# One more field by one-hot rows, pair products of a tile in one go, and gathers without marks

## The reference

```python
e  = stack([tbl_f[ids[:, f]] for f in range(26)], axis=1)        # (2048, 26, 32)
x1 = einsum('bik,bjk,hij->bhk', e,  e, W1) + b1[None, :, None]   # h = 128
x2 = einsum('bik,bjk,hij->bhk', x1, e, W2) + b2[None, :, None]
z  = sum(concat([x1, x2], axis=1), axis=-1)                      # (2048, 256)
h  = concat([z, dense_ctx], axis=1)                              # (2048, 272)
h  = maximum(h @ W_top1 + b_top1, 0)                             # 512
h  = maximum(h @ W_top2 + b_top2, 0)                             # 256
y  = h @ W_top3                                                  # (2048, 1)
```

## Time and profile before

| | us |
|---|---|
| median of 3 timed executions | 502.41 (498.45 to 503.1) |
| the profiled execution's own time | 499.69 |
| its span | 497.9 |
| PE busy | 466.3 (94%) |
| DVE busy | 387.7 (78%) |
| POOL busy | 347.6 (70%) |
| ACT busy | 254.4 (51%) |
| mean granted TensorE clock | 0.993 |

### The profile page before, as it was taken

One profiled execution on the slowest core, in us unless ns is written; L12 is line 12 of the kernel. 1 busy time (PEld: TensorE's weight loads), 2 busy tenths in 40 slices (PEclk: granted clock), 3 DMA queues, 4 the chain that ended last, 5 costly groups with the idle time before them and its releaser, 6 DMA issues.

```text
span 497.9 us, 24830 instructions
## 1 busy us (share of the span) xinstructions
PE 466.3 (94%) x10658; PEld 448.1 (90%) x10658; DVE 387.7 (78%) x1143; ACT 254.4 (51%) x531; POOL 347.6 (70%) x274
## 2 busy tenths in 40 slices
PE   4998889869799999999999999999999999999998
PEld 3887879869688998999999999999999999999997
DVE  8699959497596959795979796989779898875302
ACT  7876835375446354544554555546453545455211
POOL 5887978757888878787878787788878788810000
PEclk9999999989999999999999999999999999999999
DMA  6631031120020212020203020202021210000000
GB/s 219 170 105 15 8 66 38 36 54 19 11 65 14 60 13 62 12 58 13 62 11 62 12 58 12 59 14 56 14 34 40 38 35 11 9 5 1 3 0 3
DMA packets 14001, 19.57 MB, mean 39 GB/s; under 512 B 5123, under 2 KB 11528, under 8 KB 13838
## 3 DMA queue, kind: packets, MB, share of 16 engines
q0 software_dynamic: 8512, 4.38, 9.0%
q1 hardware_dynamic: 5454, 14.73, 8.3%
HBM read 19.08 MB, written 0.01 MB: 38 GB/s over the span
## 4 chain that ended last, share of the span: by engine, by line
PE 72%; DVE 14%; issue 4%; DMA 3%; POOL 3%; ACT 3%; SPq 0%; DVEq 0%; ACTq 0%; POOLq 0%
PE psum L939 15%; PE psum L913 15%; PE psum L958 11%; PE psum L984 8%; PE psum L892 6%; DVE work L643 6%; DVE onehot L486 5%; PE psum L1006 4%; POOL emb L396 3%; DMA emb<-in_tbl,idx 3%; PE psum L934 2%; PE psum L835 2%; PE psum L856 2%; PE psum L858 2%; PE psum L979 2%
## 5 line engine op out<-in xcount | busy, mean ns | idle before, releaser
L396 POOL DMA_INDIRECT emb<-in_tbl,idx x266 | 346.7, 1303 | 90.3 <-issue 62.3
L754 ACT COPY t_area<-psum 128x432 f32<-128x432 f32 x256 | 125.2, 541 | 98.2 <-PE psum L913 72.0
L643 DVE TENSOR_TENSOR work<-embT 128x32 f32<-128x32 f32 (+12 forms) x416 | 129.2, 386 | 0.0
L939 PE MATMUL psum<-t_area,v 128*128 (+1 forms) x992 | 113.4, 275 | 0.0
L939 PEld LDWEIGHTS psum<-t_area,v 128*128 128x128 f32 x992 | 112.1, 192 | 0.0
L913 PE MATMUL psum<-diag,work 64*64 64x54 f32 (+1 forms) x6144 | 103.5, 218 | 7.0 <-ACT diag L731 3.6
L913 PEld LDWEIGHTS psum<-diag,work 64*64 64x64 f32 (+1 forms) x6144 | 94.7, 127 | 13.5 <-issue 8.7
L731 ACT COPY diag<-embT 32x416 f32<-32x416 f32 x128 | 69.9, 546 | 29.2 <-DVE embT L625 27.6
L958 PE MATMUL psum<-table_parts,onehot 125*128 125x96 bf16 x1350 | 62.4, 206 | 5.5 <-DVE onehot L486 3.8
L580 DVE COPY t_area<-t_area 13x384 f32<-13x384 f32 (+5 forms) x160 | 61.6, 416 | 6.8 <-ACT t_area L754 5.3
L958 PEld LDWEIGHTS psum<-table_parts,onehot 125*128 125x128 bf16 x1350 | 58.2, 98 | 8.2 <-DVE onehot L486 4.6
(11 more groups left out here) (96 smaller groups left out, 433.1 us busy)
## 6 DMA issues: line engine op xcount, KB each, us to landing
ids_all<-in_short_ids SPq DMA_DIRECT2D x15, 625.0 KB
emb<-in_tbl,idx POOLq DMA_INDIRECT x266
t_area<-in_L_rec_W SPq DMA_DIRECT2D x1, 1664.0 KB, 8.6
work<-in_W_top SPq DMA_DIRECT2D x2, 512.0 KB, 11.9
onehot<-in_tbl SPq DMA_DIRECT2D x5, 156.2 KB
onehot<-in_tbl SPq DMA_DIRECT2D x5, 125.0 KB
t_area<-in_L_rec_W SPq DMA_DIRECT2D x1, 338.0 KB, 4.0
idx<-in_ids SPq DMA_DIRECT2D x1, 208.0 KB, 2.5
```

The costliest lines, as they stand in the source:

```text
L396: eng.indirect_dma_start(emb[n][:, f * K:(f + 1) * K], None, tables[f], bass.IndirectOffsetOnAxis(ap=idx[:, t * F + f:t * F + f + 1], axis=0),
L643: last = nc.vector.tensor_tensor(pairs[:, half, :, :, tri(r):tri(r) + r + 1], halves[:, g, :, 0:r + 1], halves[:, g, :, r:r + 1].broadcast ...
L754: nc.scalar.copy(dst, src).then_inc(t_out, 1)
L939: last = nc.tensor.matmul(z_ps(t)[:, NP:2 * NP], v[:, s, :], moments(slot), start=(a == 0), stop=(a == len(terms) - 1))
```

## The change

`SHORTS` goes from 10 to 11: one more field with 1,250 rows comes by one-hot rows, and 15 gathers a tile are left. Its neighbours in the sorted list are shifted, so the parts of `short_rows` have 48, 44 and 8 matmuls, 100 in all. The third part goes to bank 4 for the first tiles and otherwise to bank 5, in columns behind z.

PE's `step` no longer mixes: all 8 phases of `t_units(t)`, then the three parts of `short_rows(t+1)`, `layer1(t-3)`, `cin(t-1)`, `layer2(t-3)`. `cin` has a new wait for `rows_ready`. On DVE `make_onehot(t+1)` stands behind both halves of the pair products, and `h1_low(t-4)` stands between the halves in place of `h1_low(t-3)` at the end of the tile. On ACT `h1_move(t-3)` comes after all 16 unit copies. The marks and the semaphore `progress` are gone: the gathers of the first 13 fields of tile t start once the first transpose of tile t-2 is done, the others once the second is.

```diff
-SHORTS = 10
+SHORTS = 11
-        def rows_ps(part):
+        def rows_ps(part, t):
+            if part == 2:
+                if isinstance(t, int) and t < 3:
+                    return psum[:, 4, 0:PARTS * K]
+                return psum[:, 5, 2 * NP:2 * NP + PARTS * K]
...
@@ gpsimd
             for t in range(2, TILES):
-                eng.wait_ge(embT_ready, 2 * (t - 1))
-                lo = first if t == 2 else steps[t - 1] - later + AHEAD
-                hi = steps[t - 1] + AHEAD
-                marks = [(prep_full, n) for n in range(AFTER_V1 + 1, PREPS + 1)] if t == 2 else []
-                count = later - len(marks)
-                lo = max(lo, 0 if t == 2 else steps[t - 2] + AHEAD)
-                marks += [(progress, lo + 1 + k * (hi - lo) // count) for k in range(count)]
-                gather(t, marks)
+                for c in range(2):
+                    eng.wait_ge(embT_ready, 2 * (t - 2) + c + 1)
+                    eng.nop(nofuse=True)
+                    gather(t, c)
@@ vector, tile
-                make_pairs(t, n, (lambda: make_onehot(t + 1)) if not known or t + 1 < TILES else None)
+                make_pairs(t, n, (lambda: h1_low(t - 4)) if not known or t >= 4 else (lambda: None))
+                if not known or t + 1 < TILES:
+                    make_onehot(t + 1)
...
-                if not known or t >= 3:
-                    h1_low(t - 3)
@@ scalar, step
-                    for u in range(UNITS // 2):
+                    for u in range(UNITS):
                         unit_out(t, n, u)
                 if not known or 3 <= t < TILES:
                     h1_move(t - 3)
-                if not known or t < TILES:
-                    for u in range(UNITS // 2, UNITS):
-                        unit_out(t, n, u)
@@ tensor, cin
+                if not (isinstance(t, int) and (t == 0 or t >= TILES - 2)):
+                    eng.wait_ge(rows_ready, t + 2)
@@ tensor, short_rows
+                    if part == 2 and not (isinstance(t, int) and t < 3):
+                        eng.wait_ge(z_lo_ready, t - 2)
@@ tensor, step
-                t_units(t, 0)
+                for half in range(2):
+                    t_units(t, half)
+                if not known or t < TILES - 1:
+                    for part in range(len(ROW_PARTS)):
+                        short_rows(t + 1, part)
                 if not known or t >= 3:
                     layer1(t - 3, n)
-                t_units(t, 1)
+                if not known or t >= 2:
+                    cin(t - 1, n)
                 if not known or t >= 3:
                     layer2(t - 3)
-                if not known or t >= 2:
-                    cin(t - 1, n)
```

More of the change, by code:

```diff
@@ L384, in _, with gather @@
                 eng.iota(first_row_int[:, size:size + 1], pattern=[[0, 1]], base=0, channel_multiplier=n).then_inc(rows_known, 1)
-            def gather(t, marks):
+            def gather(t, c=None, marks=None):
                 n = t % 2
-                fields = [f for f in range(F) if f not in SHORT or t == 0]
+                fields = [f for f in range(F) if (f not in SHORT or t == 0) and c in (None, f // HF)]
                 held = None
-                for f, mark in zip(fields, marks):
+                for f, mark in zip(fields, marks or [None] * F):
                     if mark is not None and mark != held:
@@ L403, in _ @@
             later = F - SHORTS
-            gather(0, [None] * EARLY + [(prep_full, AFTER_W2T + 2 * k + 1) for k in range(HF)]
+            gather(0, None, [None] * EARLY + [(prep_full, AFTER_W2T + 2 * k + 1) for k in range(HF)]
                    + [(prep_full, AFTER_MOVED + 2 * k + 1) for k in range(F - EARLY - HF)])
             at = AFTER_MOVED + 2 * (F - EARLY - HF)
-            gather(1, [(prep_full, n) for n in range(at + 1, AFTER_V1 + 1, 2)] + [(t_full, u) for u in range(2, UNITS + 1, 2)]
+            gather(1, None, [(prep_full, n) for n in range(at + 1, AFTER_V1 + 1, 2)] + [(t_full, u) for u in range(2, UNITS + 1, 2)]
                    + [(prep_full, AFTER_V1 + 1)] * later)
-            steps = [sum(marks_in(t) for t in range(u)) for u in range(TILES)]
-            first = len(MARK_PHASES)
             for t in range(2, TILES):
-                eng.wait_ge(embT_ready, 2 * (t - 1))
-                lo = first if t == 2 else steps[t - 1] - later + AHEAD
-                hi = steps[t - 1] + AHEAD
-                marks = [(prep_full, n) for n in range(AFTER_V1 + 1, PREPS + 1)] if t == 2 else []
-                count = later - len(marks)
-                lo = max(lo, 0 if t == 2 else steps[t - 2] + AHEAD)
-                marks += [(progress, lo + 1 + k * (hi - lo) // count) for k in range(count)]
-                gather(t, marks)
+                for c in range(2):
+                    eng.wait_ge(embT_ready, 2 * (t - 2) + c + 1)
+                    eng.nop(nofuse=True)
+                    gather(t, c)
         @block.vector
@@ L492, in make_rows @@
                 for part, fields in enumerate(ROW_PARTS):
-                    eng.wait_ge(rows_full, 2 * (t - 1) + part + 1)
-                    of_field = rows_ps(part).rearrange("p (j a k) -> p j k a", a=PARTS, k=K)
-                    runs = [j for j, f in enumerate(fields) if j == 0 or fields[j - 1] != f - 1] + [PER_BANK]
+                    eng.wait_ge(rows_full, len(ROW_PARTS) * (t - 1) + part + 1)
+                    of_field = rows_ps(part, t).rearrange("p (j a k) -> p j k a", a=PARTS, k=K)
+                    runs = [j for j, f in enumerate(fields) if j == 0 or fields[j - 1] != f - 1] + [len(fields)]
                     for lo, hi in zip(runs, runs[1:]):
@@ L628, in transposes, with make_pairs @@
                 eng.wait_ge(embT_ready, 2 * t + 2)
-            def make_pairs(t, n, between=None):
+            def make_pairs(t, n, between):
                 e = embT[n][:, :, :]
@@ L634, in make_pairs @@
                 for half in range(2):
-                    if half == 1 and between is not None:
+                    if half == 1:
                         between()
@@ L666, in _ @@
             eng.wait_ge(extra_ready, 1)
[L667 removed]
+            make_pairs(0, 0, lambda: None)
             own = split_tables(1, own)
@@ L680, in _ @@
             pack(TILES - 1, 1)
+            h1_low(TILES - 4)
+            z_low(TILES - 2, 0)
             make_y(TILES - 4)
-            z_low(TILES - 2, 0)
             h1_low(TILES - 3)
@@ L870, in t_units @@
                 for v in range(half * phases // 2, (half + 1) * phases // 2):
[L871 to L874, removed]
                     if isinstance(t, int):
@@ L916, in small_units @@
                                 last.then_inc(t_full, 1)
-                    if j == 0 and v in MARK_PHASES:
-                        last.then_inc(progress, 1)
             def cin(t, n):
@@ L957, in short_rows @@
                     for c in range(chunks):
-                        last = nc.tensor.matmul(rows_ps(part)[:, j * PARTS * K:(j + 1) * PARTS * K],
+                        last = nc.tensor.matmul(rows_ps(part, t)[:, j * PARTS * K:(j + 1) * PARTS * K],
                                                 onehot[:, ONEHOT_AT[c] + o - BY_CHUNK[c], :],
@@ L1029, in _ @@
             make_v(AFTER_V1, PREPS)
-            for part in range(2):
+            for part in range(len(ROW_PARTS)):
                 short_rows(1, part)
```

18 lines of the change are left out of this document (1 added, 17 removed).

## The result

| | before | after |
|---|---|---|
| median, 4 executions each | 501.83 us | 507.84 us (505.12 to 509.08) |
| ratio | | 1.0117, 95% interval 1.0076 to 1.0158 |
| profiled execution: time, span | 499.69, 497.9 | 509.08, 506.9 |

The span of the profiled execution grew by 9.0 us, the median time by only 6.0: the changed kernel's profile shows the slowest of its four executions, and the one before is of an execution 2.1 us under its median. So the trace overstates the loss by some 3 us. PE's step starts (the first matmul of `t_units` in each tile) say where. `t_units(3)` starts at 135.7 us (135.5 before), `t_units(4)` at 167.9 (164.6), `t_units(15)` at 457.5 (448.2), and 49.4 us are left (49.7). So tile 3's step, the first of PE's loop, lost 3.1 us, the eleven steady steps (tiles 4 to 14) 6.0 us, start and end together nothing.

A forecast was written before the change was run, and what follows sets the result against it. PE was taken to set the pace, busy 278.87 of 283.6 us in eleven steps. Steady steps +13.2 and start -2.7 gave +10.5 on 499.69, 510.2, or 512.9 on the median; predicted 511.5, range 500 to 519.

The forecast's parts named there:

- Eight phases in a row: PE's t_units: waits for ACT's bank copies before phases 2, 4 and 6; +1.0 us a step, bounds +0.5 and +1.4.
- a quick and a slow kind of tile: Phases 5 to 7 before the change: five tiles at 3.34 to 3.43 us, six at 3.56 to 3.74.
- The field on PE: Ten more one-hot matmuls of 0.045 us each on PE: +0.45 us a step.
- Fewer changes of form: PE switches between quartered and whole matmuls four times less: -0.1 us a step, bounds 0 and -0.3.
- late gathers: 15 gathers without marks fit POOL into PE's step, removing late steady tiles: -0.2 us a step.
- DVE's order: DVE needs 22.8 us before PE gives the next part 0 at 24.7: 2 us to spare, no new wait bites.
- The start: Tiles 1 to 3: 7 us wait before tile 2, tile 3's step ending near 161.9; -2.7 us, bounds 0 and -5.
- The end: Tile 15 and the rest, whole matmuls in nearly the same order: nothing, bounds -1 and +1 us.
- Rival A: ACT's copies never hold PE, eight phases take 7.9 us in all: 492 to 494 us; chance 0.11.
- rival B: All tiles run phases at 9.0 us, +0.45 us a step: 502 us, 505 on the median; chance 0.19.
- Rival C: DVE sets the step if its work stretches by 3 us: each step 1 us longer, 522 us; chance 0.05.
- Rival D: POOL's gathers hang under DVE's products, needing 28.3 us a tile: 520 us; chance 0.05.

The follow-up runs named there:

- half_copy2: Changed kernel, but from tile 4 on each ACT unit copy moves only the first half of its slots (measurement only, z wrong); 499.4 us, ratio 0.9968.
- mix4: Changed kernel with two quarters of layer1 and short_rows part 0 put back between PE's phases, half of layer1 before cin; 498.3 us, ratio 0.9953.

## Why the prediction came out right, and where its sum did not

- **Eight phases in a row** (+1.0 taken, bounds +0.5 and +1.4): +0.48 measured, with the mechanism and the wait's releaser as forecast, and confirmed by half_copy2 and mix4. The first two of its three places show in the trace above, the third lies inside a merged row. I took the mean of a quick and a slow kind of tile; the changed kernel runs near the quick one, 9.2 us for the eight phases where 9.0 and 9.9 were reckoned. The middle was taken, and the truth lay at the lower bound: this is the term of the sum that was mis-sized.
- **The field on PE** (+0.45): 4.42 against 4.04 us, +0.38.
- **Fewer changes of form, late gathers** (-0.1, -0.2): neither was measured by itself. PE's waits for late one-hot columns, 2.3 us in 3 waits before, are gone, which fits the second. With these two as forecast, 0.48 + 0.38 - 0.3 = 0.56 against a measured 26.33 - 25.78 = +0.55 a step, +6.0 in eleven; forecast was +13.
- **DVE's order**: 22.8 us of work with 2 us to spare; the trace shows up to 2.7 us of waiting for part 0 (DVE, line 488). `cin` after tile 2's rows waited 0.73 us (0.8 forecast).
- **The start** (-2.7): +3.3 at tile 4. Its first part was right: a wait of 7.48 us before tile 2 (7 forecast) with a slow clock behind it, and tile 3 at 135.7 (134.8). The step that failed is "its step of 27 us ends near 161.9". It took 32.1, with 4.5 us of gaps without a releaser and 1.5 us of slow clock that the sum has no term for. That code came too slowly for eight phases packed into one stretch, in the loop's first pass, is the likely cause, by timing alone. The trace of before had a small sign of it, a gap of 0.80 us with no releaser in tile 3. The size, too, is that of one execution, the slowest of four: its mean granted clock was 0.987, that of the fastest (505.1 us) 0.993.
- **The end** (0): -0.3.
- **Rival A** (banks do not hold PE) is refuted by the 27 waits, and **rival B** (the quick kind) is nearest to the steady steps. With tile 3's loss the sum came out 1.5 us under the forecast in the profiled executions (+9.0 against +10.5). Two errors of 7 and 6 us cancelled, which was luck: the total was better than its working. On the medians it is +6.0 against a forecast of 511.5 - 502.4 = +9.1.
- **Rival C** did not occur. **Rival D**'s mechanism did: two gathers hung through both halves of the products,

```profile
80.02 8.38 POOL L392 DMA_INDIRECT emb<-in_tbl,idx  x1 [0.30 <-issue]
105.82 7.81 POOL L392 DMA_INDIRECT emb<-in_tbl,idx  x1 [0.30 <-issue]
```

and DVE then waited up to 2.3 us for tile 3's gathers, whose products released PE last (0.38 us). In the steady tiles one gather hangs 3.5 to 4.4 us under most halves of the products, and POOL has the room: a tile's 15 gathers take it some 24 us of PE's 26.3. By the Trainium skill (SBUF — State Buffer, section Who interferes with whom) a `tensor_tensor` should not keep GpSimd from writing descriptors. The page calls that inferred. Here the gathers of 7.81 and 8.38 us lie over products and, at their end, 1.1 us of line 472, with no gap on DVE. The measurement decides, with the mechanism left open.

## What to carry to other kernels

Work that stands between the phases of a producer with few buffers need not be in its way: here it was the time in which the buffers drained (mix4 gained 9.5 us by putting some of it back), so count phases in a row before moving it out. A wait that costs nothing may be covered by one neighbour, and moving the neighbour costs the whole wait (0.84 us a step here). When a change is made of several parts, time them alone: the gathers without marks gained 1%, and the rest of the change lost 2%. When a profile explains a difference, compare its own time with the median first: here 3 of its 9 us were the choice of the execution.

## What was not expected of the hardware

In a loop's first pass pieces of 0.02 MB came on the instruction queue every 3.4 to 5.1 us, and PE, working through 128 quartered matmuls with their weight loads in 2.0 to 2.5 us, stood still until 2.2 to 2.7 us after the next piece began. That it waited for this code is argued from the times, not shown by a run. With a 0.69 MB load on other queues at the same time one piece took 2.1 us instead of 1.0, and one gap was 2.69 us long. After it the granted clock was 0.50 and 100 matmuls took 5.93 instead of 4.42 us; after a gap of 2.40 us in another kernel it was not.
